# Third norm, logits and the first half's choices inside the last projection of a two-layer transformer

## The reference

```
x = x + L1_attn(layernorm(x))     # 16 heads of width 128, causal
x = x + L1_ffn(layernorm(x))      # mixture of experts

logits = xn @ gate.T                              # 64 experts
scores = softmax(logits)
groups = top_k(max of each of 8 groups of 8, 3)   # the other groups are set to 0
topk_w, topk_i = top_k(scores in these groups, 6)
pos    = running count of each expert over (row, choice), minus 1
slot   = expert * 96 + min(pos, 95)               # 96 places for each expert
buf[slot] = xn[row]
out    = (silu(buf @ Wg.T) * (buf @ Wu.T)) @ Wd.T # for each expert, width 176
y      = sum over the 6 choices of out[slot] * topk_w
shared = (silu(xn @ Sg.T) * (xn @ Su.T)) @ Sd.T   # every row, width 352
result = y + shared
```

## Time and profile before

| what | us |
|---|---|
| median of 3 runs (lowest, highest) | 1540.43 (1539.98, 1542.67) |
| the profiled execution's own time | 1539.46 |
| its span, first to last instruction | 1537.8 |
| PE busy | 1391.1 (90%) |
| DVE busy | 1042.2 (68%) |
| ACT busy | 814.9 (53%) |
| mean granted PE clock | 0.951 |

### The profile page before, as it was taken

How to read it: one execution, slowest core, us unless ns; L and a number is a source line. 1 busy time by engine, 2 the same in 40 slices (tenths; PEclk the granted TensorE clock), 3 DMA queues, 4 the chain that set the end, 5 groups by cost and what they waited for, 6 DMA issues and landing times. The chain is left out here.

```text
span 1537.8 us, 36415 instructions
## 1 busy us (share of the span) xinstructions
PE 1391.1 (90%) x12869; PEld 982.9 (64%) x12869; DVE 1042.2 (68%) x2205; ACT 814.9 (53%) x1682; POOL 356.1 (23%) x782
## 2 busy tenths in 40 slices
PE   5779999998779999999899999999989797799977
PEld 3434555555647777777686777777768735699953
DVE  7867677764878888888714888888881378422228
ACT  2336565554157878777703878777770127233320
POOL 0145665510201111111110111110101000577730
PEclk9879999999889999999999999999999799799985
DMA  3059898840037655555601766555560520699948
GB/s 103 3 141 220 253 244 227 220 103 13 1 107 144 138 134 136 134 134 138 146 20 26 138 138 139 134 133 138 132 136 17 164 66 1 187 283 289 274 153 289
DMA packets 463450, 215.08 MB, mean 140 GB/s; under 512 B 412131, under 2 KB 434497, under 8 KB 463121
## 3 DMA queue, kind: packets, MB, share of 16 engines
q1 hardware_dynamic: 449040, 175.09, 46.4%
q0 software_dynamic: 12000, 36.90, 8.2%
q10 hardware_dynamic: 2336, 2.16, 0.4%
HBM read 81.97 MB, written 31.52 MB: 74 GB/s over the span
## 5 line engine op out<-in xcount | busy, mean ns | idle before, releaser
L1080 PE MATMUL bank<-a_pt,v_part 128*128 128x128 f16 x3456 | 234.2, 219 | 15.9 <-DMA a_pt<-a_ph 11.7
L1143 ACT ACTIVATE a_ph<-a_p,a_rinv 128x1024 f16<-128x1024 f32 (+7 forms) x256 | 198.7, 777 | 80.3 <-POOL a_rinv L1022 76.1
L762 DVE TENSOR_REDUCE a_qh<-bank 128x1 f16<-128x1024 f32 (+7 forms) x256 | 182.4, 755 | 84.7 <-PE bank L652 82.2
L1080 PEld LDWEIGHTS bank<-a_pt,v_part 128*128 128x128 f16 x3456 | 207.7, 98 | 49.3 <-DVE z_part L1170 7.7
L1151 DVE TENSOR_REDUCE a_negm<-bank 128x1 f32<-128x1024 f32 (+7 forms) x256 | 192.0, 751 | 57.6 <-PE bank L1064 57.4
L1059 PE MATMUL bank<-a_k,a_q 128*128 128x512 f16 (+3 forms) x1152 | 228.6, 326 | 0.2
L750 ACT ACTIVATE a_p<-bank 128x1024 f32<-128x1024 f32 (+7 forms) x256 | 158.0, 650 | 128.9 <-PE bank L707 113.8
L1185 DVE SCALAR_TENSOR_TENSOR a_ph<-a_p,a_rinv,a_ph 128x1024 f16<-128x1024 f32 (+7 forms) x256 | 207.3, 810 | 1.7 <-ACT a_ph L1143 1.7
L1132 ACT ACTIVATE a_p<-bank,a_negm 128x1024 f32<-128x1024 f32 (+7 forms) x256 | 189.5, 740 | 21.6 <-DVE a_negm L1151 21.5
L1022 POOL TENSOR_TENSOR a_rinv<-a_rinv,p_scale 128x1 f32<-128x1 f32 x256 | 48.8, 191 | 612.6 <-DVE a_rinv L1164 612.4
L931 PE MATMUL bank<-x_part,wsplit 128*128 128x512 f16 x768 | 186.0, 379 | 4.1 <-PEq L211 1.8
(11 more groups left out here) (206 smaller groups left out, 2214.8 us busy)
## 6 DMA issues: line engine op xcount, KB each, us to landing
wgu<-in_wgu SPq DMA_DIRECT2D x64, 352.0 KB
choice_rows<-zero POOLq DMA_DIRECT2D x24, 512.0 KB, 4.1
c_rows<-choice_rows SPq DMA_DIRECT2D x16, 768.0 KB, 11.4
wsplit<-w_parts POOLq DMA_DIRECT2D x30, 384.0 KB, 3.9
...
a_pt<-a_ph SPq DMA_TRANSPOSE x256, 3.0
```

The source lines that it names most:

```text
L762: dve.tensor_reduce(qh[s][:, i, MC:MC + 1], s1_place(t), AX.X, ALU.max, negate=True).then_inc(m_ready, 1)
L1080: ins = eng.matmul(Z_ps[:, cols], g.vs[par][v_][:, k, :], turned[slot][:, a * blocks[j] + k, :], start=(k == 0 and (v_, a) == PARTS[0]), s ...
L1143: eng.activation(parts[slot][:, 0:w_], probs[slot][:, 0:w_], ACT.Copy, scale=rinv[:, p_, jj:jj + 1]).then_inc(p_hi, 1)
```

## The change

The norm block n3 and its barrier are gone. The last projection is a new block, `proj_and_choose`, which holds the norm too: tiles 0 to 7, which are final by then, are normed at once, and tiles 8 to 15 in pairs after the adds of each pair (`ROW_GROUPS`). The transposes and the logits stand between the projections of the tiles on PE. All copies into `g.xT` are ACT's now. DVE also makes softmax, groups, choices and one-hots of the first half there (class `Choose`, half 0); the router does it for the second half, on tiles half as wide. The router's order is new: PE does 7 `gate_up` steps (`AHEAD`) before it waits for `s_m` and 5 behind, the picks 0 and 1 after the last two of them, and two down projections before each of picks 2 to 5. ACT makes one half of one `at_expert` after each Silu, with six buffers. `LATE` is 8, so that 8 tiles of down projections come in the experts' block. The weights `sgu` are loaded a block earlier. The two parts of x for layer 1 share their memory with `g.xT`.

```diff
+        with ExitStack() as cm:
+            moe_buffers(g, cm)
+            with ExitStack() as c2:
+                norm(nc, g, "n2", "split", *l1_buffers(nc, g, c2))
+                l1_attention(nc, g, 0)
+                proj_out1(nc, g, 0)
+                l1_attention(nc, g, 1)
+                with ExitStack() as c3:
+                    proj_and_choose(nc, g, c3)
+            moe(nc, g, out)
...
-    g.xs = [g.sb(f"x_part{a}", [P, DC, T], F16, c2) for a in range(2)]
+    g.xs = [g.xT[:, a, :].bitcast(F16).rearrange("p (c n) -> p c n", c=DC) for a in range(2)]
...
+def moe_buffers(g, c):
+    g.xT = g.sb("xT1", [P, DC, T], F32, c)
...
+    g.sgu = g.sb("sgu", [P, DC, 2 * MS], F32, c)
+    g.sc = g.sb("scores", [P, NT, E], F32, c)
+    g.mask = g.sb("mask", [P, NT, E], BF16, c)
+    g.oh = g.sb("onehot", [P, K, NT, E], BF16, c)
+    g.iotab = g.sb("iotab", [P, C], BF16, c)
+    g.gib = g.sb("gib", [P, NT, 8], BF16, c)
+    g.n_chained = 0
...
+    def shifted(self, dve):
...
+        dve.wait_ge(self.s_lg, self.half + 1)
+        self.chained(dve, dve.tensor_reduce(mx, logits, AX.X, ALU.max))
+        dve.tensor_tensor(self.tmp[:, :, :], logits, mx.unsqueeze(2).to_broadcast([P, BT, E]),
+                          ALU.subtract).then_inc(self.s_ex, 1)
...
+    def onehot(self, dve, k):
...
+        self.chained(dve, dve.tensor_tensor(g.oh[:, k, ts, :], eid, g.gib[:, ts, k:k + 1].to_broadcast([P, BT, E]),
+                                            ALU.is_equal))
+        dve.nop().then_inc(self.s_oh, 1)
+        if k:
+            self.chained(dve, dve.tensor_tensor(g.mask[:, ts, :], g.oh[:, 0, ts, :] if k == 1 else g.mask[:, ts, :],
+                                                g.oh[:, k, ts, :], ALU.add))
...
+ROW_GROUPS = ((0, BT), (BT, BT + 2), (BT + 2, BT + 4), (BT + 4, BT + 6), (BT + 6, NT))
+def proj_and_choose(nc, g, c):
...
+            sp.dma_start(g.sgu[:, :, :], g.t["sgu"]).then_inc(g.sem("r_weights"), 16)
+            xv = g.xrows.rearrange("(n p) d -> p n d", p=P)
+            for q in range(4):
+                sp.wait_ge(s_xn, R0 + 4 * q + 4)
+                sp.dma_start(xv[:, 4 * q:4 * q + 4, :], xn[:, 4 * q:4 * q + 4, :]).then_inc(s_kept, 16)
...
+            def turn(p):
+                pe.wait_ge(s_xn, R0 + 2 * p + 2)
+                if p >= 4:
+                    pe.wait_ge(s_ev, p - 3)
+                for c_ in range(DC):
+                    for j in range(2):
+                        ins = pe.transpose(place[p % 4][:, (2 * c_ + j) * P:(2 * c_ + j + 1) * P],
+                                           xn[:, 2 * p + j, c_ * P:(c_ + 1) * P], g.identf[:, :])
+                ins.then_inc(s_tr, 1)
+            def logits(p):
+                pe.wait_ge(s_ev, p + 1)
+                for t in (2 * p, 2 * p + 1):
+                    for c_ in range(DC):
+                        ins = pe.matmul(g.bank[0][:, t // BT, (t % BT) * E:(t % BT + 1) * E],
+                                        g.xT[:, c_, t * P:(t + 1) * P], g.gate[:, c_, :],
+                                        start=(c_ == 0), stop=(c_ == DC - 1))
+                if p % (BT // 2) == BT // 2 - 1:
+                    ins.then_inc(s_lg, 1)
+            for n in range(BT):
+                if n >= 2:
+                    pe.wait_ge(s_add, N0 + n - 1)
+                for h in range(H):
+                    for a, w_ in PARTS:
+                        ins = pe.matmul(g.bank[2 + n % 2][:, 0, 0:D], g.z[a][:, h, n * P:(n + 1) * P],
+                                        g.wo1p[w_][:, h, :], start=(h == 0 and (a, w_) == PARTS[0]),
+                                        stop=(h == H - 1 and (a, w_) == PARTS[-1]))
+                ins.then_inc(s_mm, 1)
+                if n == 0:
+                    for p in range(4):
+                        turn(p)
+                elif n == 1:
+                    pe.wait_ge(s_in, 80)
+                    for p in range(4):
+                        logits(p)
+                elif n % 2 == 0:
+                    turn(3 + n // 2)
+                else:
+                    logits(3 + n // 2)
+            turn(7)
+            logits(7)
...
+            root(0)
+            for p in range(4):
+                evac(p)
+            root(1)
+            first.exponentials(act)
+            evac(4)
+            for i in range(2, 5):
+                root(i)
+                evac(3 + i)
...
+            rows(0)
+            for n in range(BT):
+                t = BT + n
+                dve.wait_ge(s_mm, N0 + n + 1)
+                dve.wait_ge(s_bo, N0 + n + 1)
+                dve.tensor_tensor(g.x[:, t, :], g.bank[2 + n % 2][:, 0, 0:D], g.x[:, t, :],
+                                  ALU.add).then_inc(s_add, 1)
+                dve.wait_ge(s_add, N0 + n + 1)
+                dve.bn_stats(g.stats[:, t, :], g.x[:, t, :]).then_inc(s_st, 1)
+                if n % 2:
+                    dve.wait_ge(s_st, ST0 + n + 1)
+                    rows(1 + n // 2)
+                if n == 1:
+                    dve.wait_ge(s_in, 80)
+                    first.chained(dve, dve.tensor_copy(g.iotab[:, :], g.iota[:, :]))
+                elif n == 2:
+                    first.shifted(dve)
+                    first.normalized(dve)
+                elif n == 3:
+                    first.groups(dve)
+                elif n == 4:
+                    first.choices(dve)
+                    first.onehot(dve, 0)
+                elif n == 5:
+                    first.onehot(dve, 1)
+                elif n == 6:
+                    for k in range(2, K):
+                        first.onehot(dve, k)
...
-LATE = 12
+LATE = 8
...
-            for n in range(len(gu_steps)):
+            for n in range(AHEAD):
                 gate_up(n)
...
-            pe.wait_ge(s_h, len(gu_steps))
-            for t in range(8):
-                shared_down(g, pe, t, hT, 0)
...
+            def pick(k):
                 pe.wait_ge(s_eh, k + 1)
                 pe.wait_ge(s_ph, k + 1)
                 for t in range(NT):
                     ins = pe.matmul(g.bank[0][0:C, 1, 0:2 * E], ph[k % 2][:, t, :],
-                                    eh[k % NEH][:, t, :, :].rearrange("p a e -> p (a e)"),
+                                    eh[k][:, t, :, :].rearrange("p a e -> p (a e)"),
                                     start=(k == 0 and t == 0), stop=(k == K - 1 and t == NT - 1))
                 ins.then_inc(s_used, 1)
+            for n in range(AHEAD, len(gu_steps)):
+                gate_up(n)
+                if n >= len(gu_steps) - 2:
+                    pick(n - len(gu_steps) + 2)
+            pe.wait_ge(s_w, 16 + 16 * NMS)
+            pe.wait_ge(s_h, len(gu_steps))
+            for k in range(2, K):
+                for t in (2 * k - 4, 2 * k - 3):
+                    shared_down(g, pe, t, hT, 0)
+                pick(k)
...
+            def at_expert(k, half):
+                ts = slice(half * BT, (half + 1) * BT)
+                if half:
+                    act.wait_ge(s_oh, K + k + 1)
+                act.activation(eh[k][:, ts, 1, :], oh[:, k, ts, :], ACT.Copy, scale=float(k + 1))
+                for t in range(half * BT, (half + 1) * BT):
+                    ins = act.activation(eh[k][:, t, 0, :], oh[:, k, t, :], ACT.Copy, scale=token[:, t:t + 1])
+                if half:
+                    ins.then_inc(s_eh, 1)
+            second.exponentials(act)
...
-            for k in range(K):
-                act.wait_ge(s_oh, k + 1)
-                if k >= NEH:
-                    act.wait_ge(s_used, k - NEH + 1)
-                act.activation(eh[k % NEH][:, :, 1, :], oh[:, k], ACT.Copy, scale=float(k + 1))
-                for t in range(NT):
-                    ins = act.activation(eh[k % NEH][:, t, 0, :], oh[:, k, t, :], ACT.Copy, scale=token[:, t:t + 1])
-                ins.then_inc(s_eh, 1)
+                at_expert(n % K, n // K)
...
+            second.shifted(dve)
+            second.normalized(dve)
+            shared(1)
+            second.groups(dve)
             shared(2)
-            chained(dve.tensor_reduce(gmx[:, :, :], sc.rearrange("p t (a b) -> p t a b", b=GS), AX.X, ALU.max))
-            for t in range(NT):
-                ins = dve.max(g8[:, t, :], gmx[:, t, :])
-            chained(ins)
-            for t in range(NT):
-                ins = dve.max_index(gi[:, t, :], g8[:, t, :], gmx[:, t, :])
-            chained(ins)
-            chained(dve.tensor_copy(gif[:, :, :], gi[:, :, :]))
-            gid = iota[:, 0:NG].unsqueeze(1).to_broadcast([P, NT, NG])
-            for k in range(TG):
-                chained(dve.tensor_tensor(gmask[:, min(k, 1)], gid, gif[:, :, k:k + 1].to_broadcast([P, NT, NG]),
-                                          ALU.is_equal))
-                if k:
-                    chained(dve.tensor_tensor(gmask[:, 0], gmask[:, 0], gmask[:, 1], ALU.add))
-            chained(dve.tensor_tensor(msc.rearrange("p t (a b) -> p (t a) b", b=GS),
```

(33 more changed lines are left out.)

244 lines of the change are left out of this document (150 added, 94 removed).

## The result

The changed kernel took 1514.28 us (median of 4 runs, 1511.05 to 1516.70) against 1541.50 us before (median of 4, 1539.98 to 1542.67): ratio 0.9828, interval 0.981 to 0.9847. The forecast was 1512.0 us in a range of 1504 to 1521. The profiled execution took 1511.05 us, with a span of 1509.4 us at a mean granted clock of 0.963 (0.951 before). 1511.0 was forecast for it.

A forecast was written before the change was run, and what follows sets the result against it. No single engine but a chain through all was taken to bound the norm and router. The first gather comes 28.5 us earlier, nothing counted behind it: 1539.46 - 28.5 = 1511.0, plus 1.0 to the median, 1512 us (1504 to 1521).

The forecast's parts named there:

- Projection block: Last projection with norm and logits inside: 1201.0 + 6.0 logits + 2.8 transposes + 2.0 clock loss, ending at 1211.8.
- I count nothing: Projection block: DVE's 39.7 us of work fit in 53, tightest at tile 3; no delay counted (up to 8 us).
- The end of the block: From the last projection to the router: 7.9 us of remaining work plus 0.3 for the engines' meeting; router starts at 1220.0.
- Router up to `s_m`: Router start to position counts: DVE decides with 27.2 us, PE's seven steps take 25.3; before, 65.2 us.
- `s_m` to the gather: PE's and DVE's lists of 38.0 us each plus 1.0 lost in waits: 39.0 us (38 to 44); before, 34.5.
- Experts' start: Eight down projections, 10.6 us, fit in the 12.3 us until rows arrive, full clock expected; counted 0 (-1.4 to +8).
- From the profile to the median: Final sum: the runs' median lies 1.0 us above the profiled execution, so 1511.0 becomes 1512.
- A: Rival: in the projection block logits pull PE's clock down and it stays down; 1561 us, chance 0.03.
- B: Rival: DVE bounds both half-wide parts, as small instructions hardly shrink; up to 8 or 12 us, 1520; chance 0.09.
- C: Rival: gain given back at the experts' start, PE cold, eight tiles up to 20 us instead of 12.3; 1520; chance 0.07.
- D: Rival: router bound by PE's steps, 63.4 us floor against 66.2; same time within 3 us; inside the forecast's 0.78.
- The table switches: Two additional Sqrt/Exp switches between tiles: the skill's 2.66 us each makes Exp 0.6 us late, the trace's 1.28 not at all.

The follow-up runs named there:

- the spare bytes: 32 bytes per partition left free behind the buffer `last`: 1517.83 us on the changed kernel, 1511.33 us on the version with adds and sums early, products later.

## Why the prediction was right, and where it was not

The mechanism was right: the time of the change is the move of the first gather, 28.3 us against 28.5 forecast, and nothing behind it gave it back. That the two agree to 0.2 us is luck: with the other profiles of either kernel the move is 27 to 32 us. By its steps:

- **Projection block.** The last projection and the logits put behind it ended 53.2 us after the block's start (1213.3), 52.9 forecast, but by two errors that cancel. The 2.0 us for the clock were not lost: PEclk is 1.00 over the whole block, the logits took half of their time before as assumed (128 in 14.40 us where they were tried, 0.11 each), and the transposes ran warm between the matmuls. In their place stand the 2.0 us that PE waited behind its first tile.
- **"I count nothing" for DVE** is the step that failed. The sum of DVE's work came out (37.2 us in the window and 2.7 behind it, 39.7 reckoned; 2.9 of it is what POOL added to the small steps), but a sum over 53 us doesn't tell of a chain of small steps that has to be done within one tile. The tight place was named as tile 3; it was tile 0, where the steps cost 0.65 us beside POOL, and again the last tile, where the add comes 1.1 us late (it begins 1.35 us after PE has gone on to the logits, and 0.26 us after that in the version in which the one-hot stands behind it).
- **The end of the block**: from there to the router 8.0 us (1213.3 to 1221.33), 8.2 forecast (7.9 + 0.3): the add begins 0.4 us late against that point, and my other terms had 0.5 us too much.
- **Router up to `s_m`**: 28.7 us, 27.2 forecast. Of the waits I had put in, the one for the first Silu was shorter (1.70 instead of 2.6), and PE and DVE waited for each other at two places that I hadn't (0.46 us before the seventh step, 0.50 before a mask). DVE decides, as forecast, but by less: PE's seven steps took 26.8 us and not 25.3, because the cold first us of the router fall on seven steps here and on twelve in the row that I divided. 4.8 us more on DVE cost 5.9.
- **`s_m` to the gather**: 37.6 us (1250.04 to 1287.68), 39.0 forecast. Two lists of equal length lost nothing by waiting for each other: PE and DVE were busy 34.1 and 32.2 of 37 us. PE's sum of 38.0 was near only by luck: PE was busy 34.3 us from `s_m` to the end of the last pick, at 1.00, where the 25.25 us that I started from ran at 0.88, and behind the last pick 2.8 us pass (1284.92 to 1287.68) in which PE has nothing to do. Both together, 66.3 us, against 66.2.
- **Experts' start**: counted as 0, with -1.4 as the lower end; in the profiled execution the clock stayed at 1.00 over 2.28 and 1.26 us of idle PE, and the stages behind the gather are 1.4 us shorter, which is within their scatter. Full clock there was luck of the execution: in three variants the same 2.28 us were followed by 0.50. The forecast rested on the 3.07 us of idle PE that had left the clock at 1.00, and these were followed by 0.50 in the repeated profile of before.
- **From the profile to the median** I carried over the 1.0 us of before. It is 3.2 after. The profiled execution was the fastest of its four; over nine runs of the unedited changed kernel the median is 1515.86 us. The second attention is where the profiles show it: 1.7 us longer in the profiled execution and 3.8 on average (724.1 against 720.3; 2.6 if only those at full clock are taken), a term that the sum did not have at all. I took everything ahead of the block for unchanged.
- **Rivals.** A fell by the quadrupled logits. B has a small part of the truth (3.1 us in the projection's block, of which 2.0 were POOL's doing). C has next to none: its cold start came in three variants and cost about half a us. D describes what would have happened with the old order, and its price of 3 us would have been wrong for it: the same halves in that order give 11 us less.
- **The table switches** cost nothing: DVE waits 0.69 us for the router's Exp, as reckoned, and the first Silu waits for its matmul (1.38 us), not for its table. The 0.6 us by which Exp would have been late by the Trainium skill ("ScalarE: Activation LUTs", What ACT_TABLE_LOAD costs) are not to be seen.

In "SBUF — State Buffer", section "SBUF: two separate sides", the Trainium skill describes such slow steps of DVE: GpSimd and VectorE share one pair of ports, which VectorE takes with two SBUF inputs or in a 2-port mode, and whichever comes first holds it for a whole instruction. Here one POOL add takes 5.50/8 = 0.69 us, and each of DVE's small steps took 0.65: it stood for about one of POOL's instructions each time, and 0.17 without them. The trace agrees in the size; that it is the ports is the page's reading, and no run here tells it from another effect of POOL's adds.

**The best version** is the one with the bias adds and half the sums early and the products later. With and without the spare bytes, which do nothing, it took 1506.22 to 1514.60 us in ten runs, median 1510.55, which is 5.3 us below the median of nine runs of the changed kernel (on other chips; both kernels' ratios to before tell them apart, 0.9801 and 0.981 against 0.9828 and 0.984).
